# Causal attention: the second normalisation moves from VectorE to ScalarE, and the inverse denominators are spread by single precision products

## The chip, the cores and the metric

The kernel runs on one core of one Trainium2 chip. The metric is the device time of one execution in microseconds (us). Engines are named as in the profile: PE is TensorE's matrix products, PEld its weight loads, DVE is VectorE, ACT is ScalarE, POOL is GpSimd, SP is SyncE.

## The reference, cut to what matters

The program is two layers, each an attention over a context followed by a feed forward part. The change touches the second layer's causal attention alone:

```python
def _layernorm(x, w, b):
    mu = jnp.mean(x, axis=-1, keepdims=True)
    var = jnp.mean((x - mu) ** 2, axis=-1, keepdims=True)
    return (x - mu) * jax.lax.rsqrt(var + EPS) * w + b
...
hidden_states = _layernorm(x)                    # without w and b
ln1_out = _layernorm(hidden_states, ln1_weight, ln1_bias)
qkv = jnp.einsum('sbh,oh->sbo', ln1_out, qkv_weight)
q, k, v = ...                                    # 16 heads of 8; 4 key and value heads, each used by 4
scores = jnp.einsum('sbhd,tbhd->bhst', q, k) * scale
probs = jax.nn.softmax(jnp.where(causal, scores, lowest), axis=-1)
attn = jnp.einsum('bhst,tbhd->sbhd', probs, v).reshape(S, B, H)
```

Here x is 32 x 128 x 128. The axis of length 32 is the sequence of this attention, the first axis of 128 its batch, the last one the features. After the attention come the projection, another normalisation and a mixture of eight experts.

## The kernel before, in words

The function attention2 is the causal stage. It handles the batch in 32 quads of four elements; a quad fills a tile of 128 rows (4 heads of a group by 32 positions) and 512 columns. Four quads make a chunk, so there are eight chunks, n = 0 to 7, and a quad q has n = q // 4 and k = q % 4. Every engine runs its own function step(q) for q from -12 up, in the order written there. Nothing else sets the order: an engine runs its instructions in turn, and semaphores (wait_ge and then_inc) tie the engines together. The first twelve steps fill the pipeline.

The path of a chunk. GpSimd adds two tiles (line 1324); VectorE takes mean and variance (stats, lines 1423 to 1432); GpSimd's prep (lines 1301 to 1309) makes the inverse roots, for the first normalisation and for the second one applied to the result of the first, which needs no more than another root of the same variance. GpSimd's hidden (line 1314) writes the first result to H. VectorE's normalise (lines 1434 to 1440, called at line 1444 for chunk 0 and at line 1501, at k = 1, for chunk n + 2) writes the second to xn with four operations of 128 x 128. TensorE's turn (line 1554, at k = 3) transposes xn into bank PX; ScalarE's high (line 1362) and VectorE's rest (line 1462) split it into two half precision parts. Then come five "slots" per chunk: TensorE's three products each (lines 95 to 97), ScalarE's hmd (line 1368), VectorE's Kc or Qd (lines 1470 and 1474). ScalarE's spread (line 1375) copies K to its place.

The path of a quad. TensorE writes scores to bank SB (lines 1620 and 1622); VectorE takes the row maxima (lines 1482 to 1488); TensorE transposes them (line 1608) into MT, which is the same bank as SB; ScalarE copies them to mc (line 1383); TensorE makes the transposed scores in bank TB (line 1611) and subtracts the maxima (line 1634); ScalarE's exponential gives Pd (line 1393); TensorE makes the values (line 1577), the product with them (line 1585) and the denominators (line 1590). TensorE may write the next scores at line 1620 only after mc has left the bank (line 1615), and ScalarE's step begins with mc and ends, at k = 2, with Pd.

The end of a chunk. At k = 0 of the next chunk VectorE takes the reciprocal Dr of the denominators (line 1509), casts it to half precision (line 1512) and subtracts to get the low part (line 1514). At k = 1 TensorE's widen (lines 1595 to 1602) spreads both parts to the rows of the output with eight selecting matrices selR, two products each; selR is made by GpSimd at line 1995, in the stage before. VectorE multiplies (Af, line 1519), and ScalarE (line 1403) and VectorE (line 1522) split the result for the projection. The last steps also prepare the first expert group, its routing among them (lines 1783 to 1822, the last operation at line 1821). A block's end waits for all engines; then experts1 begins with the products of line 95.

Of the kernel before, what the change touches and what calls it, by code (L numbers as in the profile page):

```python
# [12 lines left out]
F16 = mybir.dt.float16  # L13
BF16 = mybir.dt.bfloat16
ALU = mybir.AluOpType
ACT = mybir.ActivationFunctionType
AX = mybir.AxisListType

B, S, C, CT = 32, 128, 128, 96
# [6 lines left out]
LN_EPS = 1e-5  # L26
# [6 lines left out]
def after(eng, sem, value):  # L33

    if not isinstance(value, int) or value > 0:
        eng.wait_ge(sem, value)
# [29 lines left out]
class Room:  # L66
# [5 lines left out]
    def sb(self, name, shape, dt=F32):  # L72
        return self.ctx.enter_context(self.nc.sbuf_tensor(name, shape, dt))
# [1159 lines left out]
def attention2(nc, d, bank, keep, H, AT, wp, e):  # L1233
# [8 lines left out]
    SL = 5  # L1242
    with ExitStack() as ctx:
# [15 lines left out]
        st = sb("st2", [128, 4, 6])  # L1259
        mv = [sb(f"mv2_{i}", [128, 4, 2]) for i in range(2)]  # L1260
        rs = [sb(f"rs2_{i}", [128, 2, 2, 4]) for i in range(2)]
        xn = sb("xn2", [128, 4, C])
        xT = [sb(f"xTd{i}", [C, B * S], F16) for i in range(2)]
        hm = sb("hmd", [128, 2, 512], F16)
# [4 lines left out]
        Vq = [sb(f"Vq{i}", [128, 4, NG * HD]) for i in range(2)]  # L1269
        P = [sb(f"Pd{i}", [128, 4, 128]) for i in range(2)]  # L1270
        Dr = sb("Dr", [128, 64])
        Dh = [sb(f"Dh{i}", [128, 2, T], F16) for i in range(2)]
        Of = sb("Of", [128, 512])
        Af = sb("Af", [128, 512])
        s = room.sems("""raw wT_ready pwp_ready pT stack hi lo bias b8_ready fixed summed
            stats mv_ready root h_ready xn_ready xT_psum xT_hi xT_lo slot_psum slot_hi q_ready k_compact k_ready
            s_psum s_max m_hi m_lo mT_psum mT_ready t_psum p_ready v_psum v_ready pv_done o_sb dd_inv dd_hi dd_lo r_psum at_f at_hi at_lo""")
        PX, PJ, SB, TB, VM, O, D = bank[0], bank[1:3], bank[3], bank[4], bank[5], bank[6], bank[7]
        MT, RB = SB, PX

# [3 lines left out]
        def chunk(n):  # L1284
            return 0 <= n < G
# [9 lines left out]
        with nc.Block() as block:  # L1295
            @block.gpsimd
            def _(pool):
                pool.memset(half[:], -0.5)
                expert_constants(pool, e)

                def prep(n):
                    r, v = rs[n % 2], mv[n % 2][:, :, 1]
                    pool.wait_ge(s["mv_ready"], n + 1)
                    after(pool, s["xn_ready"], n - 1)
                    pool.tensor_scalar(r[:, 0, 0, :], v, 1.0, LN_EPS, ALU.mult, ALU.add)
                    pool.tensor_scalar(r[:, 0, 1, :], v, 1.0 + LN_EPS, LN_EPS * LN_EPS, ALU.mult, ALU.add
                                       ).then_inc(s["root"], 1)
                    pool.wait_ge(s["root"], 2 * n + 1)
                    pool.tensor_tensor(r[:, 1], r[:, 0], half[:], ALU.pow).then_inc(s["root"], 1)

                def hidden(n):
                    pool.wait_ge(s["root"], 2 * (n + 1))
                    for k in range(4):
                        last = pool.tensor_scalar(H[:, 4 * n + k, :], Xq[:, 4 * n + k, :], mv[n % 2][:, k, 0:1],
                                                  rs[n % 2][:, 1, 0, k:k + 1], ALU.subtract, ALU.mult)
                    last.then_inc(s["h_ready"], 1)

                def step(q):
                    n, k = q // 4, q % 4
                    if k == 0 and chunk(n + 3):  # L1320
                        if n + 3 == 0:
                            pool.wait_ge(keep["xq_in"], 16 * B)
                        pool.wait_ge(s["fixed"], n + 4)
                        pool.tensor_tensor(quads(Xq, n + 3), quads(Xq, n + 3), quads(Yq, n + 3), ALU.add
                                           ).then_inc(s["summed"], 1)
                    if k == 2 and chunk(n + 3):
                        prep(n + 3)
                    if k == 1 and chunk(n + 2):
                        hidden(n + 2)
                for q in range(FIRST, QUADS):  # L1330
                    step(q)
                expert_root(pool, e, 0)
                expert_sum(pool, e, Xq, H, 0)

            @block.scalar
            def _(act):
# [20 lines left out]
                act.activation(bv[:], bank[3][:, 0:1], ACT.Copy).then_inc(s["b8_ready"], 1)  # L1357
                act.wait_ge(s["b8_ready"], 3)

                def high(n):  # L1360
                    act.wait_ge(s["xT_psum"], n + 1)
                    act.activation(tok(xT[0], n), PX[:], ACT.Copy).then_inc(s["xT_hi"], 1)
# [15 lines left out]
                def step(q):  # L1378
                    n, k = q // 4, q % 4
                    if has(q):  # L1380
                        act.wait_ge(s["mT_psum"], q + 1)
                        after(act, s["t_psum"], q)
                        act.activation(mc[0:32, :], MT[0:32, 0:64].bitcast(BF16), ACT.Copy).then_inc(s["mT_ready"], 1)
                    if chunk(n + 1):
                        for i in ((0, 1), (2, 3), (4,), ())[k]:
                            slot(n + 1, i)
                    if k in (1, 2) and chunk(n + 1):
                        spread(n + 1, 2 * k - 2)
                        spread(n + 1, 2 * k - 1)
                    if has(q):  # L1390
                        act.wait_ge(s["t_psum"], q + 1)
                        after(act, s["pv_done"], q - 1)
                        act.activation(P[q % 2][:].rearrange("p a x -> p (a x)"), TB[:], ACT.Exp, scale=SCALE
                                       ).then_inc(s["p_ready"], 1)
                    if k == 0 and chunk(n - 1):
                        act.wait_ge(s["pv_done"], q)
                        after(act, s["at_f"], n - 1)
                        act.activation(Of[:], O[:], ACT.Copy).then_inc(s["o_sb"], 1)
                    if k == 3 and chunk(n + 2):
                        high(n + 2)  # L1400
                    if k == 3 and chunk(n - 1):
                        act.wait_ge(s["at_f"], n)
                        act.activation(tok(AT[0], n - 1), Af[:], ACT.Identity, bias=bv[:]).then_inc(s["at_hi"], 1)
                    if q == QUADS - 1:
                        expert_high(act, e, PJ[1], 0)
                    if q == QUADS + 1:
                        expert_exp(act, e, 0)
# [4 lines left out]
            def _(dve):  # L1412
# [18 lines left out]
                        last = dve.bn_aggr(mv[n % 2][:, k, :], st[:, k, :])  # L1431
                    last.then_inc(s["mv_ready"], 1)

                def normalise(n):
                    dve.wait_ge(s["root"], 2 * (n + 1))
                    after(dve, s["xT_psum"], n)
                    for k in range(4):
                        last = dve.tensor_scalar(xn[:, k, :], Xq[:, 4 * n + k, :], mv[n % 2][:, k, 0:1],
                                                 rs[n % 2][:, 1, 1, k:k + 1], ALU.subtract, ALU.mult)
                    last.then_inc(s["xn_ready"], 1)  # L1440

                fix(0)
                stats(0)
                normalise(0)
                fix(1)
                idv = ident[:].rearrange("p (g r x) -> p g r x", r=4, x=HD)
                dve.tensor_reduce(low[:, 0:1], idv[:, :, 2, :], AX.XY, ALU.add)
# [30 lines left out]
                def step(q):  # L1478
# [18 lines left out]
                                          ).then_inc(s["v_ready"], 1)  # L1497
                    if k == 0 and n + 3 >= 2 and chunk(n + 3):
                        fix(n + 3)
                    if k == 1 and n + 2 >= 1 and chunk(n + 2):  # L1500
                        normalise(n + 2)
                    if k == 2 and n + 3 >= 1 and chunk(n + 3):
                        stats(n + 3)
                    if k == 3 and chunk(n + 2):
# [1 line left out]
                    if k == 0 and chunk(n - 1):  # L1506
                        dve.wait_ge(s["pv_done"], q)
                        after(dve, s["r_psum"], n - 1)
                        dve.reciprocal(Dr[:], D[:, 0:64]).then_inc(s["dd_inv"], 1)
                        dve.wait_ge(s["dd_inv"], n)  # L1510
                        dr = Dr[:].rearrange("p (a s) -> p a s", s=T)
                        dve.tensor_copy(Dh[0][:], dr).then_inc(s["dd_hi"], 1)
                        dve.wait_ge(s["dd_hi"], n)
                        dve.tensor_tensor(Dh[1][:], dr, Dh[0][:], ALU.subtract).then_inc(s["dd_lo"], 1)
                    if k == 1 and chunk(n - 1):
                        dve.wait_ge(s["r_psum"], n)
                        dve.wait_ge(s["o_sb"], n)
# [15 lines left out]
            def _(pe):  # L1533
# [59 lines left out]
                    last.then_inc(s["pv_done"], 1)  # L1593

                def widen(n):
                    pe.wait_ge(s["dd_lo"], n + 1)
                    after(pe, s["xT_lo"], min(n + 3, G))
                    rv = RB[:].rearrange("p (a j s) -> p j a s", a=2, s=T)
                    for j in range(8):
                        for i in range(2):  # L1600
                            last = pe.matmul(rv[:, j], selR[:, j, :], Dh[i][:], start=(i == 0), stop=(i == 1))
                    last.then_inc(s["r_psum"], 1)

                def step(q):
# [351 lines left out]
def causal_tiles(room):  # L1956
# [1 line left out]
    tiles = {  # L1958
        "identb": sb("identb", [128, 128], BF16), "cm": sb("cm", [128, 128], BF16), "mc": sb("mc", [128, 128], BF16),
        "gm": sb("gm", [128, 32]), "gmj": sb("gmj", [128, 8, 32]), "nsel": sb("nsel", [128, 4, 128], BF16),  # L1960
        "selR": sb("selR", [128, 8, 128], F16), "w8f": sb("w8f", [C, SL, 128]),
        "K_all": sb("Kd", [128, 2 * 64 * T], F16),
    }
    tiles["K"] = [tiles["K_all"][:, 64 * T * i:64 * T * i + 64 * T].rearrange("p (n l t) -> p n l t", n=16, t=T)
# [108 lines left out]
```

## Time and profile before

| | before |
|---|---|
| time, median of 3 runs | 867.25 us (865.78 to 868.15) |
| span of the profiled execution | 862.7 us |
| its own time around the span | not shown by the profile |
| busy PE, PEld | 727.4 us (84%), 545.5 us (63%) |
| busy DVE | 639.6 us (74%) |
| busy ACT | 408.4 us (47%) |
| busy POOL | 198.2 us (23%) |
| mean granted TensorE clock | 0.931 |

The shares are averages over stages that differ. A row of the profile that begins with a line names the engine, the operation, the tile written and the tiles read, the shapes and a count; in a timeline the first two numbers are the start in us from the span's start and the time from the first start to the last end. A bracket gives the engine's idle time just before, and who ended it. The word issue there means that nothing the profile shows was waited for. A single precision product has two records. The granted clock is 1.00 at full speed.

### The profile page before, as it was taken

To read this page: it belongs to the slowest core of one execution; us is meant where nothing else is said; L and a number is where in the kernel's file an instruction comes from. 1 tells how busy PE (TensorE), PEld (TensorE's weight loads), DVE (VectorE), ACT (ScalarE), POOL (GpSimd) and SP (SyncE) were. 2 spreads that over 40 slices of the span, in tenths; PEclk is the share of its full clock that TensorE was granted. 3 is DMA by queue.
4 is the path that set the end of the run, shared out by engine and by line. 5 is a ranking of instruction groups with operands and counts; after the bars stand their busy time and mean duration, and the time that the engine had idled before them with its cause. 6 is when DMAs were issued, how large, how long until landed. Compare 5 with 4: busy or idle time off the path is not lost. (4 is left out here: it accounts for less than half of the span.)

```text
span 862.7 us, 26300 instructions
## 1 busy us (share of the span) xinstructions
PE 727.4 (84%) x10112; PEld 545.5 (63%) x10112; DVE 639.6 (74%) x1802; ACT 408.4 (47%) x777; POOL 198.2 (23%) x317
## 2 busy tenths in 40 slices
PE   3468898888888889889999477887759999999997
PEld 2245565555556777667787245665547888888886
DVE  7568877787868989888996577887665766666653
ACT  3123223322235656656655365665635555554553
POOL 3333222232534212330200553342011110011100
PEclk9569989998898999999999599999998999999999
DMA  4000000140034221122200000000000000000000
GB/s 103 9 22 13 23 21 21 33 88 18 24 99 100 82 78 50 53 66 79 81 15 14 4 2 5 5 4 4 5 3 2 13 13 0 12 12 12 12 13 13
DMA packets 33082, 26.43 MB, mean 31 GB/s; under 512 B 9740, under 2 KB 29912, under 8 KB 32984
## 3 DMA queue, kind: packets, MB, share of 16 engines
q1 hardware_dynamic: 29944, 24.07, 10.5%
q8 instruction: 70, 1.15, 0.6%
q10 hardware_dynamic: 3040, 0.98, 0.5%
q14 instruction: 28, 0.23, 0.1%
HBM read 13.51 MB, written 7.34 MB: 24 GB/s over the span
## 5 line engine op out<-in xcount | busy, mean ns | idle before, releaser
L1931 PEld LDWEIGHTS bank<-w2r,hme 128*128 128x128 f32 x1024 | 132.2, 191 | 15.6 <-ACT hme L1876 1.4
L1931 PE MATMUL bank<-w2r,hme 128*128 128x128 f32 x1024 | 135.5, 276 | 0.0
L1876 ACT ACTIVATE hme<-bank,b 128x512 f32<-128x512 f32 x128 | 86.5, 687 | 96.3 <-PE bank L97 96.3
L984 ACT ACTIVATE P<-bank 128x512 f32<-128x512 f32 x128 | 76.6, 598 | 76.2 <-PE bank L1130 75.0
L1900 DVE SCALAR_TENSOR_TENSOR Xq<-bank,wgte,Xq 128x128 f32 (+1 forms) x256 | 72.1, 344 | 51.1 <-PE bank L1931 38.3
L1056 DVE TENSOR_SCALAR bank<-bank 128x512 f32<-128x512 f32 x128 | 89.6, 700 | 15.2 <-PE bank L1121 14.4
L1064 DVE TENSOR_REDUCE mx<-bank 128x4 f32<-128x512 f32 x128 | 87.1, 681 | 1.4 <-PE bank L1104 1.3
L500 ACT ACTIVATE w2r<-bank 128x512 f32<-128x512 f32 x40 | 23.9, 597 | 114.5 <-PE bank L814 82.8
L1130 PE MATMUL bank<-mT,negsel 128*128 128x128 f16 x512 | 51.0, 223 | 13.9 <-DVE bank L1056 12.6
L95 PE MATMUL bank<-xTe,w 128*128 (+1 forms) x128 | 48.8, 381 | 5.5 <-PEq L1295 5.5
L825 PE MATMUL bank<-w_raw,hm 128*128 128x128 f32 x320 | 50.3, 308 | 2.9 <-DVE X L739 2.8
L825 PEld LDWEIGHTS bank<-w_raw,hm 128*128 128x128 f32 x320 | 45.6, 216 | 8.7 <-issue 7.1
L96 PE MATMUL bank<-xTe,w 128*128 (+1 forms) x128 | 48.8, 381 | 0.0
L97 PE MATMUL bank<-xTe,w 128*128 (+1 forms) x128 | 48.8, 381 | 0.0
L1706 POOL TENSOR_SCALAR rs<-mv 128x4 f32<-128x4 f32 x8 | 1.5, 193 | 199.8 <-DVE mv L1768 199.8
L1368 ACT ACTIVATE hmd<-bank,b8m,low 128x512 f16<-128x512 f32 x40 | 29.7, 775 | 35.8 <-PE bank L97 35.8
L1130 PEld LDWEIGHTS bank<-mT,negsel 128*128 128x128 f16 x512 | 33.1, 99 | 18.7 <-issue 13.9
L973 POOL TENSOR_TENSOR inv_sum<-inv_sum,dn 128x16 f32<-128x16 f32 x32 | 7.0, 219 | 164.6 <-DVE dn L1085 146.9
L1141 PE MATMUL bank<-P,V 128*32 128x128 f32 x1024 | 42.8, 285 | 0.2 <-ACT P L984 0.2
L416 POOL TENSOR_TENSOR rn<-n,half 128x8 f32<-128x8 f32 x8 | 13.8, 1720 | 105.8 <-DVE n L639 105.8
L95 PE MATMUL bank<-Yq,w 128*128 128x512 f16 (+1 forms) x80 | 34.2, 427 | 1.5 <-DVE hm L670 1.0
L96 PE MATMUL bank<-Yq,w 128*128 128x512 f16 (+1 forms) x80 | 33.4, 418 | 0.0
(382 smaller groups left out, 1785.3 us busy)
## 6 DMA issues: line engine op xcount, KB each, us to landing
cross_q<-qh SPq DMA_DIRECT2D x24, 128.0 KB
Q<-cross_q SPq DMA_DIRECT2D x8, 384.0 KB, 3.9
X<-in_x SPq DMA_DIRECT2D x8, 256.0 KB, 2.8
Xq<-X SPq DMA_DIRECT2D x32, 64.0 KB
cross_k<-kh SPq DMA_DIRECT2D x16, 128.0 KB
Yq<-Y SPq DMA_DIRECT2D x32, 64.0 KB
out_x<-Xq SPq DMA_DIRECT2D x32, 64.0 KB, 1.7
cload<-in_ctx SPq DMA_DIRECT2D x8, 192.0 KB, 2.5
```

The source lines that it names most:

```text
L95: pe.matmul(ps, lhs[0], rhs[0], start=start, stop=False, **kw)
L96: pe.matmul(ps, lhs[0], rhs[1], start=False, stop=False, **kw)
L97: return pe.matmul(ps, lhs[1], rhs[0], start=False, stop=stop, **kw)
L825: last = pe.matmul(DN[:, cols], hm[:, p, cols], w_raw[:, 2, p, :], start=(p == 0 and i == 0), stop=(p == NBLK - 1), skip_group_check=True)
L984: act.activation(P[j][:], TB[u % 3][:], ACT.Exp, scale=SCALE).then_inc(s["p_ready"], 1)
L1056: dve.tensor_scalar(TB[(U * b + j) % 3][:], TB[(U * b + j) % 3][:], -CLIP, CLIP, ALU.max, ALU.min).then_inc(s["t_clip"], 1)
L1064: dve.tensor_reduce(mx[:, 4 * j:4 * j + 4], SB[j % 2][:].rearrange("p (h k) -> p h k", h=4), AX.X, ALU.max).then_inc(s["s_max"], 1)
L1130: last = pe.matmul(TB[(U * b + j) % 3][:, cols(h)], negsel[:, 4 * j + h, :], mT[:], start=False, stop=True, skip_group_check=True)
L1141: last = pe.matmul(O[32 * h:32 * h + 32, cols(j)], V[b // 4 % 2][:, b % 4, 4 * h + j, :], P[j][:, cols(h)], start=True, stop=True, tile_po ...
L1876: act.activation(hm[:, p % HR], UP[p % RING][:], ACT.Gelu_apprx_tanh, bias=b1[:, p:p + 1]).then_inc(s["gelu"], 1)
L1900: last = dve.scalar_tensor_tensor(x, Y[f % 2][:, 128 * i:128 * i + 128], w, x, ALU.mult, ALU.add)
L1931: last = pe.matmul(Y[f % 2][:, cols], hm[:, p % HR, cols], w2r[:, p], start=(p % 2 == 0 and i == 0), stop=(p % 2 == 1), skip_group_check=True)
```

## The change

ScalarE's new normalise computes scale times input plus bias, with the inverse root as scale and minus the mean times the inverse root as bias; GpSimd's prep makes that bias with two more operations, and the semaphore root counts three per chunk instead of two. ScalarE calls it for chunk 0 after the constants of the stage, and for chunk n + 2 at k = 2, behind the exponential. VectorE's normalise is gone. The reciprocal Dr is used as it is: VectorE's cast and subtraction are gone, selR is single precision, and widen makes one product for each of the eight matrices.

```diff
@@ gpsimd, prep(n) and hidden(n)
                     pool.tensor_scalar(r[:, 0, 0, :], v, 1.0, LN_EPS, ALU.mult, ALU.add)
-                    pool.tensor_scalar(r[:, 0, 1, :], v, 1.0 + LN_EPS, LN_EPS * LN_EPS, ALU.mult, ALU.add
+                    pool.tensor_scalar(r[:, 0, 1, :], v, 1.0 + LN_EPS, LN_EPS * LN_EPS, ALU.mult, ALU.add)
+                    pool.tensor_scalar(less_mean[n % 2][:, 0], mv[n % 2][:, :, 0], -1.0, None, ALU.mult
                                        ).then_inc(s["root"], 1)
-                    pool.wait_ge(s["root"], 2 * n + 1)
+                    pool.wait_ge(s["root"], 3 * n + 1)
                     pool.tensor_tensor(r[:, 1], r[:, 0], half[:], ALU.pow).then_inc(s["root"], 1)
+                    pool.wait_ge(s["root"], 3 * n + 2)
+                    pool.tensor_tensor(less_mean[n % 2][:, 1], less_mean[n % 2][:, 0], r[:, 1, 1, :], ALU.mult
+                                       ).then_inc(s["root"], 1)
...
@@ scalar
                 act.wait_ge(s["b8_ready"], 3)
 
+                def normalise(n):
+                    act.wait_ge(s["root"], 3 * (n + 1))
+                    after(act, s["xT_psum"], n)
+                    for k in range(4):
+                        last = act.activation(xn[:, k, :], Xq[:, 4 * n + k, :], ACT.Identity,
+                                              bias=less_mean[n % 2][:, 1, k:k + 1], scale=rs[n % 2][:, 1, 1, k:k + 1])
+                    last.then_inc(s["xn_ready"], 1)
+                normalise(0)
+
...
                         act.activation(P[q % 2][:].rearrange("p a x -> p (a x)"), TB[:], ACT.Exp, scale=SCALE
                                        ).then_inc(s["p_ready"], 1)
+                    if k == 2 and n + 2 >= 1 and chunk(n + 2):
+                        normalise(n + 2)
                     if k == 0 and chunk(n - 1):
...
@@ vector
-                def normalise(n):
...
                 stats(0)
-                normalise(0)
                 fix(1)
...
-                    if k == 1 and n + 2 >= 1 and chunk(n + 2):
-                        normalise(n + 2)
...
                         dve.reciprocal(Dr[:], D[:, 0:64]).then_inc(s["dd_inv"], 1)
-                        dve.wait_ge(s["dd_inv"], n)
-                        dr = Dr[:].rearrange("p (a s) -> p a s", s=T)
-                        dve.tensor_copy(Dh[0][:], dr).then_inc(s["dd_hi"], 1)
-                        dve.wait_ge(s["dd_hi"], n)
-                        dve.tensor_tensor(Dh[1][:], dr, Dh[0][:], ALU.subtract).then_inc(s["dd_lo"], 1)
@@ tensor, widen(n)
-                    pe.wait_ge(s["dd_lo"], n + 1)
+                    pe.wait_ge(s["dd_inv"], n + 1)
                     after(pe, s["xT_lo"], min(n + 3, G))
                     rv = RB[:].rearrange("p (a j s) -> p j a s", a=2, s=T)
                     for j in range(8):
-                        for i in range(2):
-                            last = pe.matmul(rv[:, j], selR[:, j, :], Dh[i][:], start=(i == 0), stop=(i == 1))
+                        last = pe.matmul(rv[:, j], selR[:, j, :], Dr[:].rearrange("p (a s) -> p a s", s=T),
+                                         start=True, stop=True)
@@ causal_tiles
-        "selR": sb("selR", [128, 8, 128], F16), "w8f": sb("w8f", [C, SL, 128]),
+        "selR": sb("selR", [128, 8, 128]), "w8f": sb("w8f", [C, SL, 128]),
```

## Rows read from the trace of the kernel before

**Rows 1.** The chain that ended last, in order of time: start us, us, what.
```profile
648.88 0.58 PE bank L95
...
830.76 0.89 PE bank L1931 x8
```
**Rows 2.** Windows: length, busy us (count) of PE, PEld, DVE, ACT, POOL, PEclk, DMA.
```profile
545.50:562.30 16.80, 13.96 (x542) 10.19 (x542) 14.80 (x41) 10.78 (x21) 6.55 (x9) 1.00 0.02 5
...
579.00:597.60 18.60, 14.37 (x539) 10.44 (x540) 14.32 (x42) 10.65 (x21) 8.06 (x11) 1.00 0.02 4
```
**Rows 3.** Timeline of ScalarE: start us, us, engine line op out<-in, shapes, count.
```profile
551.82 0.60 ACT L1393 ACTIVATE Pd<-bank 128x512 f32<-128x512 f32 x1
552.31 0.25 ACT L1383 ACTIVATE mc<-bank 32x128 bf16<-32x128 bf16 x1
554.05 0.60 ACT L1393 ACTIVATE Pd<-bank 128x512 f32<-128x512 f32 x1 [1.49 <-PE bank L1634]
...
564.30 0.60 ACT L1393 ACTIVATE Pd<-bank 128x512 f32<-128x512 f32 x1
564.80 0.25 ACT L1383 ACTIVATE mc<-bank 32x128 bf16<-32x128 bf16 x1
```
**Rows 4.** Timeline of TensorE in that chunk, with a row of weight loads.
```profile
552.75 0.38 PE L1620 MATMUL bank<-Kd,Qd 128*128 128x128 f16 x4
...
562.25 0.52 PEld L1601 LDWEIGHTS bank<-Dh,selR 128*128 128x128 f16 x16 [0.47 <-DVE Dh L1514]
562.26 0.64 PE L1601 MATMUL bank<-Dh,selR 128*128 128x64 f16 x16
...
562.73 0.39 PE L1634 MATMUL bank<-mc,nsel 128*128 128x128 bf16 x4
...
564.29 0.23 PE L1608 MATMUL bank<-identb,m 128*128 128x128 bf16 x1
...
565.19 0.38 PE L1620 MATMUL bank<-Kd,Qd 128*128 128x128 f16 x4
```
**Rows 5.** Waits of TensorE, 528.8 to 614.6 us: us in total, times, longest us.
```profile
PE bank L1620 <- ACT mc L1383: 5.5, 11, 0.7
```
**Rows 6.** Line 1608, all 32 runs: what its engine waited for, us, times.
```profile
  DVE m L1488: 0.6, 2
```
**Rows 7.** Timeline of VectorE in that chunk.
```profile
561.00 0.93 DVE L1512 CAST Dh<-Dr 128x64 f16<-128x64 f32 x1
...
564.81 1.10 DVE L1438 TENSOR_SCALAR xn<-Xq,mv,rs 128x128 f32<-128x128 f32 x4
```
**Rows 8.** Groups of ScalarE by line and shape: busy us, mean ns | idle before.
```profile
L1368 ACT ACTIVATE hmd<-bank,b8m,low 128x512 f16<-128x512 f32 x40 | 29.7, 775 | 35.8 <-PE bank L97 35.8
...
L1362 ACT ACTIVATE xTd<-bank 128x512 f16<-128x512 f32 x8 | 4.7, 593 | 7.3 <-PE bank L1554 7.3
...
L1348 ACT ACTIVATE wvr<-wT 128x128 f32<-128x128 f32 x1 | 0.3, 293 | 0.0
```
**Rows 9.** Timeline of TensorE's weight loads, two rows with a wait named issue.
```profile
520.38 0.21 PEld L1590 LDWEIGHTS bank<-Pd,gmj 128*32 128x32 f32 x13 [1.71 <-issue]
...
590.00 0.27 PEld L1590 LDWEIGHTS bank<-Pd,gmj 128*32 128x32 f32 x19 [1.74 <-issue]
```
**Rows 10.** Timeline of TensorE in the stage before, at products with one column.
```profile
445.94 1.00 PE L1112 MATMUL bank<-ln_b,w1r 128*128 128x1 f32 x8
446.80 0.22 PE L1184 MATMUL bank<-ident,m 128*128 128x128 f16 x1
```
**Rows 11.** Timeline of VectorE at the end of the stage.
```profile
643.48 0.69 DVE L1519 TENSOR_TENSOR Af<-Of,bank 128x512 f32<-128x512 f32 x1
...
648.00 0.18 DVE L1821 COPY wgte<-sele 128x32 f32<-128x32 f32 x1
```
**Rows 12.** Timeline of the start of the stage.
```profile
483.97 1.12 DVE L1438 TENSOR_SCALAR xn<-Xq,mv,rs 128x128 f32<-128x128 f32 x4 [2.33 <-POOL rs L1309]
...
488.42 1.12 PE L1554 MATMUL bank<-ident,xn 128*128 128x128 f32 x4 [5.17 <-DVE b8m L1457]
```
**Rows 13.** Windows, one stretch; columns as in rows 2.
```profile
522.00:523.00 1.00, 1.00 (x4) 0.31 (x3) 0.93 (x3) 0.00 (x0) 0.00 (x0) 0.50 0.06 16
```

More of the change, by code:

```diff
@@ L1261, in attention2 @@
         rs = [sb(f"rs2_{i}", [128, 2, 2, 4]) for i in range(2)]
+        less_mean = [sb(f"less_mean{i}", [128, 2, 4]) for i in range(2)]
         xn = sb("xn2", [128, 4, C])
@@ L1271, in attention2 @@
         Dr = sb("Dr", [128, 64])
-        Dh = [sb(f"Dh{i}", [128, 2, T], F16) for i in range(2)]
         Of = sb("Of", [128, 512])
@@ L1276, in attention2 @@
             stats mv_ready root h_ready xn_ready xT_psum xT_hi xT_lo slot_psum slot_hi q_ready k_compact k_ready
-            s_psum s_max m_hi m_lo mT_psum mT_ready t_psum p_ready v_psum v_ready pv_done o_sb dd_inv dd_hi dd_lo r_psum at_f at_hi at_lo""")
+            s_psum s_max m_hi m_lo mT_psum mT_ready t_psum p_ready v_psum v_ready pv_done o_sb dd_inv r_psum at_f at_hi at_lo""")
         PX, PJ, SB, TB, VM, O, D = bank[0], bank[1:3], bank[3], bank[4], bank[5], bank[6], bank[7]
@@ L1305, in prep @@
                     pool.tensor_scalar(r[:, 0, 0, :], v, 1.0, LN_EPS, ALU.mult, ALU.add)
-                    pool.tensor_scalar(r[:, 0, 1, :], v, 1.0 + LN_EPS, LN_EPS * LN_EPS, ALU.mult, ALU.add
+                    pool.tensor_scalar(r[:, 0, 1, :], v, 1.0 + LN_EPS, LN_EPS * LN_EPS, ALU.mult, ALU.add)
+                    pool.tensor_scalar(less_mean[n % 2][:, 0], mv[n % 2][:, :, 0], -1.0, None, ALU.mult
                                        ).then_inc(s["root"], 1)
-                    pool.wait_ge(s["root"], 2 * n + 1)
+                    pool.wait_ge(s["root"], 3 * n + 1)
                     pool.tensor_tensor(r[:, 1], r[:, 0], half[:], ALU.pow).then_inc(s["root"], 1)
+                    pool.wait_ge(s["root"], 3 * n + 2)
+                    pool.tensor_tensor(less_mean[n % 2][:, 1], less_mean[n % 2][:, 0], r[:, 1, 1, :], ALU.mult
+                                       ).then_inc(s["root"], 1)
                 def hidden(n):
-                    pool.wait_ge(s["root"], 2 * (n + 1))
+                    pool.wait_ge(s["root"], 3 * (n + 1))
                     for k in range(4):
@@ L1432, in stats @@
                     last.then_inc(s["mv_ready"], 1)
-                def normalise(n):
[L1435 to L1440, printed above, removed]
                 fix(0)
                 stats(0)
-                normalise(0)
                 fix(1)
```

## The prediction

> **What bounds the kernel now.** I read the chain of waits first, for the end of the run: from 648.88 us on it runs through the products of one engine, TensorE, in the expert stage [rows 1]. Nothing of the change lies there, so the question is how much earlier or later the causal stage before it ends. The busy time by stretch of that stage comes next: a steady chunk of four quads takes 16.8 us, and TensorE is busy for 13.96 of it, VectorE for 14.80, ScalarE for 10.78 [rows 2]. No engine is full, so the pace is a loop of waits, and the fullest engine need not be in it. The timelines show the loop. ScalarE ends the exponentials of a quad (the tile Pd), then copies the transposed maxima (mc); only after that copy may TensorE write the next scores (line 1620), because both share a PSUM bank; after the scores come the slot products or the line 1634 products, and these release ScalarE again [rows 3, 4]. Line 1620 waited for mc in 11 of the 20 steps between 528.8 and 614.6 us, 5.5 us in all [rows 5]. VectorE feeds the loop only through the maxima that line 1608 transposes, and that line waited for VectorE 0.6 us in 2 of its 32 runs [rows 6]. So ScalarE and TensorE set the pace by turns, and VectorE, the busiest, does not.
>
> **Part 1: four normalisations per chunk leave VectorE.** They cost VectorE 1.10 us per chunk [rows 7]. By the reading above that frees time that nobody waits for. After them VectorE has the Af product, whose reader on ScalarE runs two steps later. I credit nothing in the steady chunks.
>
> **Part 2: the same four arrive on ScalarE,** after Pd of the third quad of a chunk (k=2) and ahead of mc of the fourth. No row shows this form (128x128 from SBUF, scale and bias both read per partition). Lower bound: a plain copy of that size, 0.293 us. The two pointer operands are priced by line 1368 against line 1362, both 128x512 from PSUM: 0.775 less 0.593, 0.182 us. That makes 0.475 us, the value I take, since it has the size and the operands [rows 8]. Neighbours on ScalarE overlap by about 0.1 us (Pd lasts 0.60, the next starts 0.49 later [rows 3]), so four take 4 x 0.375 = 1.5 us of the queue; the lower bound gives 4 x 0.19 = 0.8, and no overlap 1.9. Queued behind them: mc, which starts at 552.31 now and would start at 553.81. It lasts 0.25 and line 1620 follows some 0.15 later (an estimate from the spacing in these rows): 554.2 instead of 552.75 [rows 3, 4], so 1.45 us later. ScalarE's idle 1.49 us ahead of the next Pd does not cover this, since that idle is the wait for TensorE's line 1634, which comes after line 1620.
>
> The Trainium skill (ScalarE: Activation LUTs, Rules for kernel authors) says to multiply and add on VectorE and not on ScalarE, VectorE being up to three times as fast in bf16. This case's rows, in single precision, put the gap at 0.475 against about 0.28 per piece; by the page's three times the pieces would be over 0.8 us, the term that follows would double to some +12, and the sum would be 885.
>
> The stage has six such steps. In two of them TensorE stands still afterwards for nothing that the profile shows (the rows say issue): 1.71 us before 520.38 and 1.74 before 590.00 [rows 9]. I take that for instructions still on their way, and if they arrive at the same time as now they hide a delay of 1.45 ahead of them. So four steps pay: **4 x 1.45 = +5.8 us**. If all six pay it is 8.7; with the lower bound 4 x 0.75 = 3.0.
>
> **Part 3: the inverse denominators.** VectorE loses the cast (0.93 us beside a GpSimd sum [rows 7]) and the subtraction after it. TensorE's weight loads for line 1601 waited 0.47 us for them in this chunk [rows 4]; the product before covered most of that, and I credit 0.15. In exchange, 16 half precision products, which now take 0.47 us from their start to that of line 1634 [rows 4], become 8 in single precision. A single precision product shows as two records with two weight loads: line 1112, four products with 128x128 weights and one column, has eight records from 445.94 to 446.80, 0.107 us each [rows 10]. Even one column costs that, so the weight load sets it. Sixteen records make 16 x 0.107 = 1.7 us. A lower bound takes 64 columns at half the 0.111 us that line 1931 needs for 128 (0.89 us for 8 records, [rows 1]): 0.9 us; an upper one adds both: 2.6.
>
> So lines 1634 and 1608 come 1.7 - 0.47 - 0.15 = 1.1 us later. Pd does not: it starts at 564.30 behind ScalarE's own copies, and line 1634 would end at about 564.25. But the transpose at 564.29 moves to 565.4, mc (now 564.80, 0.28 us of slack) to 565.7, and line 1620 to about 566.1 instead of 565.19 [rows 3, 4]: 0.9 us. Walking the other five chunks gives 0.65 to 1.1, so **6 x 0.85 = +5.1 us**. At the lower bound the 0.28 swallows nearly all of it.
>
> The last two chunks spread without slots or copies beside them. There the delay is bare: about 1.2 us each, **+2.4 us**. In the last one VectorE's Af product waits for it, and behind that in VectorE's queue stands the routing, whose last operation at 648.00 us [rows 11] ends the stage 0.9 us before the expert products begin [rows 1].
>
> **Part 4: the start of the stage.** VectorE now waits 2.33 us for the roots and normalises for 1.12 before it reaches the weights' low halves and b8m, for which TensorE waits until 488.42 [rows 12]. This goes (-3.4), but normalise(0) now runs on ScalarE after b8m and before the same transposes (+1.6, four pieces and their tail). Normalise(1) falls between ScalarE's last K copy and the second chunk's transposes; with the slack there I count +0.3 (between 0 and 1.5). Together **-1.5 us**, bounds -2.5 (the four pieces at 0.9 in all, nothing for the second) and -0.3 (1.5 for the second).
>
> **At nothing:** GpSimd's two small operations per chunk, which run a chunk before their reader while GpSimd waits for VectorE; selR in single precision, written once by GpSimd in the stage before; semaphore counts.
>
> **Sum:** 5.8 + 5.1 + 2.4 - 1.5 = +11.8 us. The profiled span is 862.7 us, the median of the runs 867.25; the profile does not show the 4.55 us around the span, and I leave them unchanged: **879.0 us**.
>
> **Rivals.** *A, VectorE sets the pace* (faster). In the steady chunks VectorE has the highest busy share [rows 2]. If the maxima that line 1608 transposes came last, the 1.10 and 0.93 us taken off would be gained in some five chunks, 10.2 us, with parts 2 and 3 inside the waits; with the start -1.5 and the last two chunks +2.4 that gives 858 us. It decides as soon as line 1608 waits for VectorE; the 0.6 us [rows 6] speak against it. 8%.
>
> *B, columns and not weight loads price the spreading.* Then line 1601 takes 0.9 us, the 5.1 falls to about 0.5 and the 2.4 to 0.9: 867.25 + 5.8 + 0.5 + 0.9 - 1.5 = 873 us. The one-column products [rows 10] speak against it. 15%. The Trainium skill (FP8 and Floating Point Precision, TensorE Precision Notes) counts true single precision as four passes through the array, which against the two half precision products of now would double line 1601 and so lead to this rival; the one-column row shows another limit.
>
> *C, the clock falls.* TensorE's gap between k=2 and k=3 grows by 1.45 us. After the still stand before 520.38 its granted clock was 0.50 at 522 to 523 us, the level of 1.2 GHz [rows 13]. If six chunks each lost another 1.5 us so: 888 us. Against it: after the equal gap before 590.00 that stretch kept 1.00 [rows 2, 9]. 10%.
>
> *D, no change that can be told.* Both unknown forms at their lower bounds, 3.0 + 0.5 + 0.9 - 1.5 = +2.9, and a little more hidden by instruction waits. 5%. The rest, 62%, is the forecast.
>
> **How the numbers follow.** The range takes in the forecast with its bounds (all six steps paid: 882; dearer weight loads: some 885) and rival B: 871 to 886. A and D, most of C stay out, which is about 2 in 10. About 0.3%, 2.6 us, is what a measurement of this kernel can tell from no change. Faster 0.08, same 0.05, slower 0.87.
>
> **What would show it.** In the changed profile, line 1620 of every fourth quad should wait for mc with the four normalisations right ahead of it on ScalarE, about 1.5 us in all; line 1601 should have 16 records some 0.107 us apart; steady chunks should take about 19 us, of which VectorE has some 12.5; TensorE should start its first transposes of the stage about 2 us sooner after the stage's start; the expert stage should be as long as now. Wrong would be: chunks at or under 16.8 us (A), line 1601 at 0.9 us (B), a granted clock under 1.00 after 530 us (C).

## The result, and the profile after

The changed kernel takes 886.51 us (median of 4 runs, 886.07 to 887.57) against 866.51 for the kernel before on the same chip: a ratio of 1.0243, 95% interval 1.0219 to 1.0268. It is slower, as forecast, but by some 20 us instead of 11.8, and half a microsecond above the range's upper end. The profiled execution took 886.07 us, its span is 884.2.

Three boundaries divide the 21.5 us between the two spans. The stage's first operation on ScalarE stands at 479.06 us instead of 477.23; 2.0 us of lag are already there in the attention before it, at 255 us, where the edit touches nothing (in the traces of the experiments below that operation stands anywhere from 476.4 to 483.2 us). The stage itself, from that operation to the table load with which ScalarE opens the expert stage (668.95 and 648.70), takes 189.9 us instead of 171.5: **18.4 us**. The rest, 1.25 us, lies behind it. The expert stage opens at a granted clock of 0.50 in both runs, and stays there for 2.85 us before and 5.33 us after; the first 5.33 us of it hold 31 products before and 22 after (windows as in [rows 2], before first):

```profile
648.70:654.03 5.33, 5.15 (x31) 3.52 (x32) 1.94 (x9) 3.30 (x4) 0.20 (x2) 0.73 0.02 3
668.95:674.28 5.33, 5.14 (x22) 2.84 (x23) 1.94 (x9) 2.66 (x3) 0.20 (x2) 0.50 0.01 3
```

The 2.48 us more at half the clock make 1.24. This does not follow the change: over the traces of the experiments below the 0.50 lasts from 2.83 us (`e4_norm_in_idle`, where this last part takes 213.97 us, before 213.98) to 6.16 us (`e5_two_pieces`, 215.60 us). So the causal stage is what has to be explained, and it is read best from the copies mc on ScalarE, one per quad. ScalarE's timeline of after, from k=2 to the next chunk, where [rows 3] shows mc 0.49 us behind Pd:

```profile
557.15 0.78 ACT L1381 ACTIVATE hmd<-bank,b8m,low 128x512 f16<-128x512 f32 x1 [1.43 <-PE bank L97]
557.95 1.28 ACT L1388 ACTIVATE Kd<-Kc 32x512 f16<-32x512 f16 x2
559.25 0.60 ACT L1406 ACTIVATE Pd<-bank 128x512 f32<-128x512 f32 x1
559.88 1.65 ACT L1368 ACTIVATE xn<-Xq,less_mean,rs 128x128 f32<-128x128 f32 x4
561.43 0.25 ACT L1396 ACTIVATE mc<-bank 32x128 bf16<-32x128 bf16 x1
564.10 0.60 ACT L1406 ACTIVATE Pd<-bank 128x512 f32<-128x512 f32 x1 [2.43 <-PE bank L1633]
565.07 0.72 ACT L1418 ACTIVATE AT<-Af,bvd 128x512 f16<-128x512 f32 x1
```

The four normalisations stand between Pd and mc, and mc comes 2.18 us behind Pd instead of 0.49: 1.69 later. From there to the next Pd it takes 2.67 us instead of 1.74, although nothing was added in that stretch. TensorE's timeline of the same chunk says why:

```profile
551.91 1.89 PE L1599 MATMUL bank<-Dr,selR 128*128 128x64 f32 x16
553.64 0.39 PE L1633 MATMUL bank<-mc,nsel 128*128 128x128 bf16 x4
...
558.41 0.23 PE L1607 MATMUL bank<-identb,m 128*128 128x128 bf16 x1
559.90 0.40 PE L1610 MATMUL bank<-Qd,Kd 128*128 128x128 f16 x4 [1.27 <-ACT Pd L1406]
561.78 0.58 PE L1619 MATMUL bank<-Kd,Qd 128*128 128x128 f16 x4 [1.47 <-issue]
562.15 0.63 PE L1621 MATMUL bank<-cm,identb 128*128 128x512 bf16 x1
562.58 1.06 PE L1553 MATMUL bank<-ident,xn 128*128 128x128 f32 x4
563.43 0.63 PE L1633 MATMUL bank<-mc,nsel 128*128 128x128 bf16 x4
```

Line 1599 (1601 before) shows 16 records in 1.89 us, and line 1633 follows its start by 1.73: 0.108 us each, against 0.47 us from start to start in [rows 4]. Line 1619 (1620 before) starts 0.10 us behind the end of mc; its wait is put down to issue, but mc is what came last. Behind it the products take longer: the scores 0.58 instead of 0.38 us, line 1621 0.63 instead of 0.38, four transposes 1.06 instead of 0.60. The windows (columns as in [rows 2]) give the clock, for a whole chunk and for the stretch behind line 1619:

```profile
545.63:565.68 20.05, 16.19 (x539) 12.56 (x539) 12.59 (x34) 12.38 (x25) 6.87 (x10) 0.91 0.02 4
...
561.50:565.00 3.50, 3.22 (x99) 2.79 (x103) 1.04 (x3) 1.07 (x4) 1.39 (x2) 0.52 0.00 0
```

A steady chunk takes 20.05 us instead of 16.7 (from mc to mc), VectorE's part falls from 14.80 [rows 2] to 12.59, and the clock falls to its 1.2 GHz level once per chunk (near 522, 542, 563, 584, 605 and 625 us), each time behind a gap of 1.47 or 1.48 us ahead of line 1619 with another of 0.7 to 1.3 us shortly before it. Before, only the first of the two was there; TensorE's timeline of the kernel before, at k=2 of such a chunk:

```profile
552.47 0.40 PE L1611 MATMUL bank<-Qd,Kd 128*128 128x128 f16 x4 [1.30 <-ACT Pd L1393]
```

Summed from mc to mc over the stage (before and after), the 18.4 us are:

| part of the stage | before | after | difference |
|---|---|---|---|
| start, to mc of the second quad (k=1) | 29.73 | 30.26 | +0.5 |
| k=1 to k=2, five chunks with a spread | 24.38 | 28.38 | +4.0 |
| k=2 to k=3, six chunks (normalisation) | 25.79 | 35.82 | +10.0 |
| k=3 to k=0, six chunks (clock) | 23.30 | 26.34 | +3.0 |
| rest, up to the sixth spread | 32.08 | 31.92 | -0.2 |
| sixth spread | 4.81 | 5.71 | +0.9 |
| from there to the table load | 31.38 | 31.46 | +0.1 |

### The profile page after: what moved, and what is told of

Same layout as the page of the kernel before. It is cut to its first block and busy times, and to the rows that moved or that the text cites. A ratio compares the mean times of both kernels' runs of the same rounds, so it can differ in the third digit from the quotient of the medians.

```text
span 884.2 us, 26300 instructions
## 1 busy us (share of the span) xinstructions
PE 749.1 (85%) x10112; PEld 563.4 (64%) x10112; DVE 625.0 (71%) x1754; ACT 421.2 (48%) x809; POOL 201.6 (23%) x333
## 5 line engine op out<-in xcount | busy, mean ns | idle before, releaser
L1056 DVE TENSOR_SCALAR bank<-bank 128x512 f32<-128x512 f32 x128 | 88.8, 694 | 16.3 <-PE bank L1121 15.6
L1488 DVE TENSOR_REDUCE mxd<-bank 128x16 f32<-128x512 f32 x32 | 22.0, 689 | 23.0 <-PE bank L1621 22.9
L416 POOL TENSOR_TENSOR rn<-n,half 128x8 f32<-128x8 f32 x8 | 13.8, 1719 | 107.5 <-DVE n L639 107.5
L95 PE MATMUL bank<-Yq,w 128*128 128x512 f16 (+1 forms) x80 | 35.1, 438 | 1.4 <-DVE hm L670 1.0
```

The lines of the kernel that those rows point to most:

```text
L95: pe.matmul(ps, lhs[0], rhs[0], start=start, stop=False, **kw)
L1056: dve.tensor_scalar(TB[(U * b + j) % 3][:], TB[(U * b + j) % 3][:], -CLIP, CLIP, ALU.max, ALU.min).then_inc(s["t_clip"], 1)
```

## Experiments

The theory before the first run had two parts: mc is late by what stands ahead of it in ScalarE's queue, and the longer stand still of TensorE brings the clock down. The rival put the clock down to the single precision products. Times are medians; ratios are to the kernel before, run on the same chip (863.97 us for the first four, 864.33 for the next four, 866.48 for the last two).

**Each half alone.** `e1_norm_only` is the changed kernel with the two half precision parts of the inverse denominators restored:

```diff
+ dve.tensor_copy(Dh[0][:], dr)
+ dve.tensor_tensor(Dh[1][:], dr, Dh[0][:], ALU.subtract)
- pe.matmul(rv[:, j], selR[:, j, :], Dr[:], start=True, stop=True)
+ for i in range(2): pe.matmul(rv[:, j], selR[:, j, :], Dh[i][:], start=(i == 0), stop=(i == 1))
```

> ScalarE normalises as in the changed kernel; the inverse denominators are split and spread in half precision as before. Theory 1 (the four pieces hold mc back by some 1.6 us in six chunks, and the still stand that this leaves on TensorE lets its granted clock fall, which costs another 0.9 us each time): the clock still falls to 0.50 once in each of these chunks, and only the 4.9 us of the spread go: 881 to 882 us. Theory 2 (the long single precision weight loads of the spread make the clock fall): the clock stays at 1.00 in the steady chunks, 876 to 877 us.

`e2_spread_only` is the kernel before with the reverse of this diff.

> VectorE normalises as before; the inverse denominators are spread in single precision. Theory 1: no fall of the clock in the steady chunks, each 0.9 us longer, the last two nearly free: 871 to 872 us. Theory 2: the clock falls in each chunk with a spread: 876 to 877 us.

The first took 879.22 us, ratio 1.0156 (1.0136 to 1.0177); the second 871.01, ratio 1.0070 (1.0045 to 1.0095). By the ratios that is 13.5 and 6.0 us, together 19.5 of the 21.1 that 2.43% make; by the medians it is 15.3 and 7.0, together 22.3 of 20.0. The local delays are those of the changed kernel (5.96 us from k=2 to k=3 in the first, 5.66 to 5.78 from k=1 to k=2 in the second; 5.97 and 5.67 in the changed kernel). So the halves add, to within the 2 us or so that these times can tell. The windows show the clock: a stretch of the normalisation alone, and then the steady 130 us of the spread alone.

```profile
562.00:568.00 6.00, 4.70 (x133) 3.98 (x134) 1.84 (x5) 3.14 (x8) 2.25 (x4) 0.51 0.01 3
```

```profile
510.00:640.00 130.00, 108.24 (x4022) 84.05 (x4020) 93.37 (x257) 75.32 (x140) 37.07 (x47) 1.00 0.02 4
```

The clock falls with the normalisation on ScalarE and half precision products, and stays with single precision ones. The rival falls. The spread alone takes 17.54 us per chunk, 0.83 more than before.

**The gap filled.** `e3_gap_filled` is the changed kernel with products that no result uses, written to unused columns, ahead of the wait for mc at k=3:

```diff
+ if has(q) and k == 3 and chunk(n + 2):
+     for _ in range(8): pe.matmul(D[:, 128:512], identb[:], cm[:] three times over)
```

> The changed kernel, with eight additional products of 128x384 into an unused part of a PSUM bank at k=3, between line 1610 and the wait for mc, where TensorE now stands still for 1.47 us; nothing reads them. Theory 1: the clock stays at 1.00 in the steady chunks and each of the six chunks wins about 0.9 us back: 880 to 882 us. Theory 2, and a third by which the clock is beside the point and the scores wait for something else: the clock falls as before or the time does not come down, 886 to 888 us.

It took 880.70 us, ratio 1.0162 (1.0129 to 1.0196), less than the changed kernel's for all the added work. TensorE's timeline, and the window over 120 us:

```profile
556.54 0.40 PE L1610 MATMUL bank<-Qd,Kd 128*128 128x128 f16 x4 [1.21 <-ACT Pd L1406]
556.77 1.46 PE L1614 MATMUL bank<-cm,identb 128*128 128x384 bf16 x8
558.42 0.38 PE L1623 MATMUL bank<-Kd,Qd 128*128 128x128 f16 x4 [0.18 <-issue]
```

```profile
520.00:640.00 120.00, 102.19 (x3523) 76.58 (x3521) 76.48 (x197) 74.95 (x145) 33.36 (x49) 1.00 0.02 4
```

The first gap stays (1.21 us), the second is closed, the clock never falls, and the scores take 0.38 us again. Chunks take 19.03 us, so the clock costs 20.05 - 19.03 = 1.0 per chunk, and the delay of mc 19.03 - 17.54 = 1.5. Over the six chunks the trace gains 9.3 us, since some stalls named issue go as well, but behind the last of them TensorE then waits 7.3 us in 5 stalls named issue, where the changed kernel has 2.3 in 3: part of the gain is given back there.

**The same operations, elsewhere in the queue.** `e4_norm_in_idle` moves them, two behind mc at k=1 and two behind mc at k=2, where ScalarE waited for TensorE; `e6_idle_and_split` does so with the half precision spread.

```diff
  act.activation(mc[0:32, :], ...)
+ if k in (1, 2) and n + 2 >= 1 and chunk(n + 2): normalise(n + 2, (2 * k - 2, 2 * k - 1))
...
- if k == 2 and n + 2 >= 1 and chunk(n + 2): normalise(n + 2)
```

> The changed kernel with ScalarE's four pieces moved: two right behind mc at k=1 and two right behind mc at k=2, where ScalarE waits 1.43 us for the slot products anyway. Theory 1: mc of the fourth quad is no longer held back, the clock stays at 1.00, and the 12 to 13 us that the six chunks lost between their third and the next second quad go: 873 to 875 us. Theory 2: the clock still falls at the spread: 878 to 879 us.

> The normalisation by ScalarE right behind mc at k=1 and k=2, and the inverse denominators split into two half precision parts as before the change. Theory (only the place in ScalarE's queue costs; the same four operations are free where ScalarE waits for TensorE): chunks of 16.7 us, the run within 0.4% of the kernel before, about 865 to 868, granted clock 1.00 in the steady chunks. Rival (ScalarE's time counts wherever it is spent, or VectorE without the normalisation is worth something): chunks of 17.5 us and more and 871 or above for the first, under 862 for the second.

They took 872.41 us, ratio 1.0088 (1.0064 to 1.0113), and 865.86, ratio 1.0021 (0.9999 to 1.0043). ScalarE's timeline of the first:

```profile
551.75 0.27 ACT L1397 ACTIVATE mc<-bank 32x128 bf16<-32x128 bf16 x1 [0.75 <-PE bank L1608]
552.04 0.88 ACT L1368 ACTIVATE xn<-Xq,less_mean,rs 128x128 f32<-128x128 f32 x2
553.45 0.78 ACT L1382 ACTIVATE hmd<-bank,b8m,low 128x512 f16<-128x512 f32 x1 [0.53 <-PE bank L97]
```

The pieces take 0.88 us out of a wait of 1.43 and the next operation starts when it would have. Steady chunks are 17.54 us with the single precision spread and 16.7 with the old one, both as without the normalisation; the clock stays up throughout in the first, and falls once in the second, behind a stall named issue of 1.64 us, as before the change. Only the place cost anything; VectorE's relief was worth nothing that these times can tell.

**Half the dose.** `e5_two_pieces` is the changed kernel with two pieces back on VectorE:

```diff
  scalar, normalise(n)
- for k in range(4):
+ after(act, s["half_ready"], n)
+ for k in range(2 if n else 0, 4):
@@ vector, step: normalise(n) there is pieces 0 and 1
+ if k == 1 and n + 2 >= 1 and chunk(n + 2): normalise(n + 2)
```

> The changed kernel with two of the four normalisations of a chunk back on VectorE (ahead of its statistics of the next chunk) and two left on ScalarE behind the exponentials of k=2; the first chunk's four stay on ScalarE. Theory (mc is late by what stands ahead of it in ScalarE's queue): mc comes some 0.75 us later than before the change instead of 1.55, so a steady chunk takes 17.54 + 0.75 = 18.3 us as long as the granted clock stays at 1.00, and the run some 4 us less than the kernel with filled gaps, about 877; if the clock still falls once a chunk, 19.3 us and about 882. Rival (a fixed price for any such instruction there, such as a change of function on ScalarE between the exponentials and the copy): 19 us or more with the clock at 1.00, as with four.

876.77 us, ratio 1.0144 (1.0102 to 1.0185). From k=2 to k=3 it takes 5.21 us: 0.93 more than before, against 1.69 for four, so 0.38 per piece and some 0.17 once; the fixed price of the rival can be no more than that. TensorE's timeline in a chunk whose clock fell, then in one where it stayed at 1.00, and the window behind the former:

```profile
535.06 0.40 PE L1621 MATMUL bank<-Qd,Kd 128*128 128x128 f16 x4 [0.73 <-ACT Pd L1407]
536.16 0.38 PE L1630 MATMUL bank<-Kd,Qd 128*128 128x128 f16 x4 [0.71 <-issue]
...
554.19 0.40 PE L1621 MATMUL bank<-Qd,Kd 128*128 128x128 f16 x4 [1.27 <-ACT Pd L1407]
555.29 0.38 PE L1630 MATMUL bank<-Kd,Qd 128*128 128x128 f16 x4 [0.71 <-issue]
```

```profile
536.00:540.00 4.00, 3.83 (x130) 3.36 (x130) 1.40 (x5) 1.98 (x5) 2.33 (x5) 0.58 0.02 4
```

With the shorter second gap the clock falls in two chunks of six: in the one of the rows at 535 us, whose gaps are the shortest of the six, and in one whose gaps, 1.30 and 0.71 us, are no longer than those of the first chunk, where it stayed. The one chunk with neither a fall nor a stall named issue takes 18.3 to 18.4 us, as forecast. So the second gap brings the fall on (closed, it never came; shortened, it came twice), but when it does is not settled by the length of the gaps alone.

**The start of the stage.** `e8_first_on_vector` is the changed kernel with normalise(0) on VectorE as before; `e10_negation_last` has GpSimd's negation behind the power:

```diff
+ pool.tensor_tensor(r[:, 1], r[:, 0], half[:], ALU.pow)
  pool.tensor_scalar(less_mean[n % 2][:, 0], mv[n % 2][:, :, 0], -1.0, None, ALU.mult)
- pool.tensor_tensor(r[:, 1], r[:, 0], half[:], ALU.pow)
```

> The changed kernel with the first chunk's normalisation back on VectorE, all else as changed. Theory (GpSimd's small operations set the first roots, so moving this one normalisation gains the first transposes next to nothing): the first turn stands 11.0 to 11.6 us behind the first operation of the stage on ScalarE (10.4 in the changed kernel, 11.2 in the one before), the first mc 25.5 to 26.5 us behind it, and the run within 1 us of the changed kernel. Rival (ScalarE's first normalisation is what the start of the stage loses by): the first mc as before the change, 25.4 us or sooner, and 1 us or more gained.

> The changed kernel with GpSimd's negation of the means moved behind the power, so that it no longer stands ahead of the roots. Theory (at the start of the stage GpSimd's small operation lasts 0.90 us only because it runs beside a VectorE operation that began first; the power behind it waits): the power starts some 0.9 us sooner behind the statistics, the negation takes about 0.2 us by then, and the product of roots and means ends 0.6 to 0.9 us sooner (7.6 to 7.9 us behind the stage's first ScalarE operation instead of 8.5). Rival (the operation is slow by itself, or the power is slowed instead): the product ends at 8.3 us or later. The run as a whole within 2 us of the changed kernel.

The first took 885.91 us, ratio 1.0249 (1.0199 to 1.0299): no different from the changed kernel. Its first turn stands 11.77 us behind the stage's first ScalarE operation and its first mc 27.12, later than I expected of either theory. So the move to ScalarE did gain 1.4 us at the first turn (10.40; the sum had 1.8); but the kernel before has 11.19 there: its roots end 6.71 us behind the stage's start (483.94 us), where the changed kernel has the product of roots and means at 8.51 (487.57). GpSimd's timeline of after, VectorE's, and GpSimd's of the kernel with the negation last and of the one with the first normalisation on VectorE:

```profile
484.64 0.90 POOL L1307 TENSOR_SCALAR less_mean<-mv 128x4 f32<-128x4 f32 x1
485.62 1.67 POOL L1310 TENSOR_TENSOR rs<-rs,half 128x8 f32<-128x8 f32 x1
487.37 0.20 POOL L1312 TENSOR_TENSOR less_mean<-less_mean,rs 128x4 f32<-128x4 f32 x1
```

```profile
484.57 0.87 DVE L1457 SCALAR_TENSOR_TENSOR w<-w8f,ln_w,w 128x640 f16<-128x640 f32 x1
```

```profile
484.79 2.31 POOL L1309 TENSOR_TENSOR rs<-rs,half 128x8 f32<-128x8 f32 x1
487.08 0.23 POOL L1310 TENSOR_SCALAR less_mean<-mv 128x4 f32<-128x4 f32 x1
487.39 0.20 POOL L1313 TENSOR_TENSOR less_mean<-less_mean,rs 128x4 f32<-128x4 f32 x1
```

```profile
483.20 0.24 POOL L1307 TENSOR_SCALAR less_mean<-mv 128x4 f32<-128x4 f32 x1
483.52 1.67 POOL L1310 TENSOR_TENSOR rs<-rs,half 128x8 f32<-128x8 f32 x1
485.27 0.20 POOL L1312 TENSOR_TENSOR less_mean<-less_mean,rs 128x4 f32<-128x4 f32 x1
```

VectorE, free of its wait, now starts line 1457 while GpSimd works on the roots. The negation beside it takes 0.90 us, and 0.23 when it is moved away, as expected; but then the power meets line 1457 and takes 2.31 instead of 1.67. The product ends 8.23 us behind the stage's start instead of 8.51, but from GpSimd's first operation on the statistics (483.90 and 483.77 us) it is 3.69 instead of 3.80: 0.1 gained, not 0.6 to 0.9. The expectation was right on the cause, that GpSimd loses beside VectorE, and wrong that the power would escape it. The last rows show the same operations while VectorE waits for them: 0.24, 1.67 and 0.20 us, and 2.79 from GpSimd's first operation to the end of the product instead of 3.80. So VectorE's work beside them costs 1.0 us. (The one time of `e10_negation_last`, 889.33 us, says nothing of a difference that small.)

**The other copies moved as well.** If what stands ahead of mc costs, ScalarE's own copies do too. `e7_copies_in_idle` is the kernel before with Of, Kd and AT right behind mc; `e9_copies_and_norm` adds the normalisation on ScalarE, behind mc at k=0.

```diff
  act.activation(mc[0:32, :], ...)
@@ the second kernel alone
+ if k == 0 and n + 2 >= 1 and chunk(n + 2): normalise(n + 2)
@@ both: Of from the end of k == 0, K's spreads from behind the slots, AT from the end of k == 3
+ if k == 1 and chunk(n - 1): act.activation(Of[:], O[:], ACT.Copy)
+ if k in (1, 2) and chunk(n + 1): spread(n + 1, 2 * k - 2); spread(n + 1, 2 * k - 1)
+ if k == 3 and chunk(n - 1): act.activation(tok(AT[0], n - 1), Af[:], ACT.Identity, bias=bv[:])
```

> The kernel before, with ScalarE's other work that stands ahead of the next maxima moved to where ScalarE waits for TensorE: the copy of O goes from the end of k=0 to right behind mc at k=1, K's spreads from behind the slots to right behind mc at k=1 and k=2, the last addition (AT) from the end of k=3 to right behind mc at k=3. Theory (a chunk is as long as the loop of ScalarE and TensorE, and each instruction taken from ahead of mc shortens it): chunks of 15 to 16.2 us, the run at 854 to 862. Rival (the steps are paced by something else, TensorE's own instructions or their supply, or the slots that now come later): chunks of 16.6 to 17.5 us, 865 to 872.

> The kernel with ScalarE's copies behind mc, and the normalisation of the change on ScalarE as well, all four of a chunk right behind mc at k=0, where ScalarE still waited 1.45 us for the slot products; half precision spread. With the copies moved, TensorE's scores at k=3 waited 0.64 us for Qd on VectorE, so VectorE is now late once a chunk. Theory (an operation taken off VectorE pays only where VectorE is what is waited for, and costs nothing on ScalarE where ScalarE waits): chunks of 15.3 to 15.9 us instead of 16.04, the run 1 to 4 us below the kernel with moved copies alone, about 857 to 860. Rival (TensorE's instructions and their supply floor the chunk at some 16 us): no difference, or more and longer waits named issue, 861. Other rival (the slots at k=0 come late behind the pieces): 862 to 866.

861.20 us, ratio 0.9969 (0.9943 to 0.9996), and 863.33, ratio 0.9963 (0.9945 to 0.9981). Both are faster than the kernel before, by a third of a per cent and barely clear of noise, and not to be told from each other. From chunk 1 on, from mc to mc at k=0, five chunks of the first take 15.6 to 17.2 us and one with long stalls 19.7, against 16.2 to 18.2 before; 15 to 16.2 was hoped for. TensorE's waits of the first, 510 to 610 us:

```profile
PE bank L1590 <- issue: 6.5, 7, 1.6
PE bank L1620 <- ACT mc L1383: 4.2, 20, 0.2
PE bank L1585 <- issue: 2.2, 4, 0.8
```

No wait for mc is longer than 0.2 us now, against up to 0.7 in [rows 5], and none for Pd is left; the stalls named issue are, 8.7 us in these two lines against 6.5 before. The second kernel's extra step gained nothing, as its first rival said: TensorE's stalls remained, and GpSimd's roots now came late:

```profile
573.62 1.65 ACT L1369 ACTIVATE xn<-Xq,less_mean,rs 128x128 f32<-128x128 f32 x4 [1.28 <-POOL less_mean L1313]
```

## Why the prediction was right and where it failed

**What sets the pace: right.** ScalarE and TensorE by turns; VectorE lost 2 us of work per chunk and nothing came of it (rival A falls, by `e6_idle_and_split` too).

**Part 2, the price of a piece: right; its place in the queue: slightly short.** The median piece takes 0.478 us (0.475 forecast), and four follow each other in 1.55. The first starts 0.63 us behind Pd's start instead of 0.49, so it does not overlap Pd: mc is 1.69 us late, not 1.45 to 1.5. The Trainium skill (ScalarE: Activation LUTs, What ACT_TABLE_LOAD costs) gives 186 ns, 0.833 ns per column and 93 ns per pointer operand, by which an estimate for this form is 479 ns; the trace, with 478, agrees.

**Part 2, two steps of six at nothing: half right.** "If they arrive at the same time as now they hide a delay of 1.45 ahead of them." They did arrive so, or nearly: the stall of 1.60 us at 520.38 (TensorE's products) is 0.46 at the same instructions in the changed kernel, that of 1.62 at 590.00 is 0.80. The first of them, before and after:

```profile
520.38 0.33 PE L1590 MATMUL bank<-Pd,gmj 128*32 128x32 f32 x14 [1.60 <-issue]
...
524.31 0.33 PE L1589 MATMUL bank<-Pd,gmj 128*32 128x32 f32 x14 [0.46 <-issue]
```

But the two steps, from mc at k=2 to mc at k=1 of the next chunk, are 0.8 and 2.2 us longer, where I had nothing: 1.69 each came ahead of stalls that gave back 1.1 and 0.8, and the clock took its own. The other four steps are 2.4 to 2.5 us longer each, 9.9 in all, where I had 5.8.

**Rival C, a chance of 10%: it came true beside the forecast, and this is the step that failed most.** The clock should have been a term of the sum. I set the new gap against one gap of equal length before 590.00 that had cost no clock [rows 2, 9], and did not see that at k=2 TensorE already stood still for 1.30 us, waiting for Pd, shortly ahead of it. The change made two gaps in a row of one. All six chunks fell, at 1.0 us each by `e3_gap_filled` (the rival had 1.5). That the second gap is at work is shown by filling it; that it needs the first ahead of it is not, since no run has the second alone.

**Part 3: right per spread, wrong at the end.** 0.108 us per record, 0.83 to 0.90 us per spread in five of six, 4.9 us in all (5.1 forecast); rival B falls. The last two cost 0.1 instead of 2.4: mc to mc at the first of them grew from 3.75 to 4.39 us, and the next step shrank from 3.84 to 3.30; TensorE's waits named issue between the sixth spread and the expert stage fell from 4.8 us to 2.3. The last spread still shows as 0.7 us more between the last mc and the table load. A delay ahead of such a stall is not bare.

**Part 4: right on the wait removed, wrong in the sum.** I charged GpSimd's added operations at nothing because they "run a chunk before their reader". That holds in the loop and not for the first chunk, where ScalarE waits for them: from the stage's start to the roots' product it takes 1.8 us more, of which 0.6 are the added operations, 1.0 VectorE's work beside them, and 0.2 later statistics. So the first turn comes 0.8 us sooner (10.40 instead of 11.19) and not 1.8. The rest of the gain goes at normalise(1), to which the sum gave +0.3: the transposes of the second chunk now wait 0.57 us for it (before, then after).

```profile
500.90 0.61 PE L1554 MATMUL bank<-ident,xn 128*128 128x128 f32 x4
...
503.19 1.11 PE L1553 MATMUL bank<-ident,xn 128*128 128x128 f32 x4 [0.57 <-ACT xn L1368]
```

From the first turn to this one it takes 13.73 us instead of 12.48, 1.25 more, and 13.6 to 13.8 in every kernel that has the four pieces of normalise(1) at that place (12.2 to 12.5 where VectorE makes it). The second mc is then 0.5 later instead of 1.5 sooner.

**The 4.55 us around the span: a wrong reading that costs nothing.** It is the median of the runs less the span of one run. In every run of this record, time and span differ by about 2 us. The forecast is a difference added to the median, so it stays as it is.

Measured against forecast: normalisation with the clock 12.9 (5.8; rows three and four of the table, and -0.2 of the rest), spread 4.9 (5.1), last two 0.1 (2.4), start 0.5 (-1.5): 18.4 against 11.8.

## What to carry to other kernels

Work handed to an engine with idle time costs what is queued behind it: four operations cost 13 us ahead of the copy that TensorE waits for, and next to nothing right behind that copy, where the engine stood waiting anyway. Before a gap of TensorE is lengthened, look for the gaps beside it: a gap of 1.5 us behind one of 0.7 to 1.3 came with a fall of the clock in every chunk, where the first alone had not. A stall named issue is neither a cover nor a fixed cost: added waits swallow it, and removed waits bring it back.

## What was not expected of the hardware

- The granted clock fell to 0.50 (1.2 GHz) in the changed kernel behind gaps of 1.21 to 1.28 and 1.47 or 1.48 us with 0.4 us of products between them in four chunks, and in the other two with 0.96, or 0.68 and 0.42, for the first; in `e5_two_pieces` behind 1.30 and 0.71 in one chunk and not in another, and behind 0.73 and 0.71 once. With the second gap closed it never fell. Stalls named issue of 1.60 us (the kernel before, at 520.38) and 1.64 us (`e6_idle_and_split`) stood ahead of a fall; others of 1.62 us (the kernel before, at 590.00) and of 1.62, 1.63 and 1.76 us (`e3_gap_filled`, behind 634 us) did not. What decides between equal gaps stays open.
- A GpSimd operation on 128x4 elements took 0.90 us instead of 0.23 beside VectorE's line 1457, and ended 0.10 us behind it. The Trainium skill (SBUF — State Buffer, SBUF: two separate sides) says that the two engines share a pair of ports as an exclusive lock, with a VectorE operation that has two inputs in SBUF among those that take it against a GpSimd one that reads there, and the later one blocked until the earlier instruction ends; these rows agree, line 1457 having two such inputs.
- Single precision products of 128x128 weights with 64 columns take 0.108 us per record, two records each, the same as with one column [rows 10].
